# A two-layer transformer block on one core: attention operands in 64 rows a head, max and exp scores on opposite row halves, causal mask by extra rows, eight heads per value bank

## The reference

```python
x = x + 0.5 * moe(layernorm(x))          # 8 experts, top 2, capacity 193 a sequence
x = x + attention(layernorm(x))          # below
x = x + 0.5 * moe(layernorm(x))

q, k, v = x @ Wq + bq, x @ Wk + bk, x @ Wv + bv      # 16 heads of 8 columns
scores = q k^T / sqrt(8) + slope[head] * -|kpos - qpos|
scores = where(kpos > qpos, -inf, scores)
out = softmax(scores) v @ Wo + bo
```

## Time and profile before

| What | Value |
|---|---|
| median of 3 runs | 1056.23 us (1055.88 to 1057.18) |
| the profiled execution, first to last instruction | 1056.2 us |
| TensorE busy | 954.3 us, 90% |
| DVE busy | 776.1 us, 73% |
| ACT busy | 660.2 us, 63% |
| POOL busy | 603.5 us, 57% |
| attention, first score matmul to last value matmul | 192.6 to 885.0 us |

### The profile page before, as it was taken

One profiled execution on the slowest core, in us unless ns is written; L12 is line 12 of the kernel. 1 busy time (PEld: TensorE's weight loads), 2 busy tenths in 40 slices (PEclk: granted clock), 3 DMA queues, 4 the chain that ended last, 5 costly groups with the idle time before them and its releaser, 6 DMA issues. The chain is left out here.

```text
span 1056.2 us, 26705 instructions
## 1 busy us (share of the span) xinstructions
PE 954.3 (90%) x6880; PEld 501.3 (47%) x6880; DVE 776.1 (73%) x2596; ACT 660.2 (63%) x1570; POOL 603.5 (57%) x1220
## 2 busy tenths in 40 slices
PE   5999993689999989989998998999999996899997
PEld 2444441345555545455554554554555543444443
DVE  5999983677677767767876876776677732799996
ACT  4767763146676746657666675675666674577675
POOL 3777775236646635556464563654646343477777
PEclk9999996799999989999999998999999999899999
DMA  6500001434223223141231421323224001010011
GB/s 170 129 0 0 0 0 44 112 86 121 66 57 103 78 66 91 36 117 53 70 91 47 107 76 48 91 63 90 78 45 112 11 1 22 11 31 21 29 30 40
DMA packets 78828, 64.50 MB, mean 61 GB/s; under 512 B 9818, under 2 KB 78426, under 8 KB 78426
## 3 DMA queue, kind: packets, MB, share of 16 engines
q1 hardware_dynamic: 78734, 63.19, 22.8%
HBM read 33.54 MB, written 29.36 MB: 60 GB/s over the span
## 5 line engine op out<-in xcount | busy, mean ns | idle before, releaser
L1062 DVE TENSOR_REDUCE att_neg_max<-att_max 128x1 bf16<-128x384 f32 (+3 forms) x704 | 424.1, 640 | 164.0 <-PE att_max L865 163.8
L960 ACT ACTIVATE att_probs<-att_exp 128x512 f32<-128x512 f32 x640 | 358.7, 598 | 224.8 <-PE att_exp L883 223.7
L1026 POOL TENSOR_SCALAR_AFFINE_SELECT att_probs<-att_probs 128x256 f32<-128x256 f32 (+1 forms) x640 | 229.9, 363 | 314.3 <-ACT att_probs L960 306.3
L862 PE MATMUL att_max<-att_k_st,att_q_st 114*128 114x128 bf16 (+3 forms) x1024 | 278.5, 310 | 34.2 <-DMA att_k_st<-qk_parts 15.7
L883 PE MATMUL att_exp<-att_q_st,att_k_st 116*128 116x256 bf16 (+3 forms) x1024 | 245.6, 303 | 1.1 <-ACT att_probs L960 1.0
L865 PE MATMUL att_max<-bf_consts 128*128 128x128 bf16 x1024 | 200.3, 225 | 0.0
L862 PEld LDWEIGHTS att_max<-att_k_st,att_q_st 114*128 114x128 bf16 x1024 | 101.1, 99 | 202.9 <-issue 84.6
L900 PE MATMUL att_pv<-att_probs,att_v 128*32 128x512 f32 (+3 forms) x2048 | 191.6, 446 | 1.2 <-POOL att_probs L1026 1.2
L344 ACT ACTIVATE moe_scaled<-moe_hi,moe_gates 128x128 f32<-128x128 f32 x512 | 146.1, 372 | 59.3 <-PE moe_hi L290 58.9
L504 DVE SCALAR_TENSOR_TENSOR x<-moe_lo,moe_gates,x 128x128 f32 (+1 forms) x512 | 160.5, 338 | 18.9 <-PE moe_lo L284 17.9
L284 PE MATMUL moe_lo<-moe_we,moe_hT 128*128 128x512 f32 x256 | 135.1, 610 | 0.0
(11 more groups left out here) (77 smaller groups left out, 923.1 us busy)
## 6 DMA issues: line engine op xcount, KB each, us to landing
qk_parts<-att_parts SPq DMA_DIRECT2D x192, 128.0 KB, 2.3
att_q_st<-qk_parts SPq DMA_DIRECT2D x32, 384.0 KB, 3.9
att_k_st<-qk_parts SPq DMA_DIRECT2D x64, 192.0 KB, 4.3
x<-in_L_attn_x SPq DMA_DIRECT2D x16, 256.0 KB, 3.0
out<-x SPq DMA_DIRECT2D x16, 256.0 KB, 2.3
att_k_st<-zero_rows SPq DMA_DIRECT2D x4, 384.0 KB
moe_we<-in_L_ffn_We SPq DMA_DIRECT2D x2, 512.0 KB, 4.3
att_q_st<-att_shift SPq DMA_DIRECT2D x64, 4.0 KB, 2.9
```

What stands on the lines that cost most here:

```text
L862: nc.tensor.matmul(max_ps[m % RING][:, c * width:(c + 1) * width], q_st[par][0:MAX_K, r, i * P:(i + 1) * P], k_st[par][ab][0:MAX_K, r, 0:w ...
L960: nc.scalar.activation(probs[g % 2][:, n, :], exp_ps[m % RING][:], ACT.Exp).then_inc(exp_done, 1)
L1026: nc.gpsimd.affine_select(out=view, in_=view, compare_op=ALU.is_ge, fill=0.0, base=0, pattern=[[0, len(blocks)], [1, P]], channel_multipli ...
L1062: nc.vector.tensor_reduce(neg_max[par][:, g // 2, ab:ab + n_ab, r0:r0 + n_r, i].rearrange("p a r -> p r a"), max_ps[m % RING][:, 0:len(hea ...
```

## The change

Each head gets 64 rows of its own: 48 of parts, 3 of position, 11 for the mask inside a diagonal block, 1 for the mask of later blocks, 1 for the maximum. The even heads stand in partitions 0 to 63 and the odd ones in 64 to 127 of q_st, and of the two stacks k_max and k_exp. The 11 and 1 mask rows are built of powers of two, so that the identity matmul goes; max scores ahead of the diagonal block are a matmul with 51 rows, those of the diagonal block one with 62, and exp scores have 64. A group now is four heads of one side: in group g the exp pass takes side g % 2 and the max pass the other side. The units run from the widest to the narrowest. The values of the two sides of a head pair stand 16 columns apart in a 32-wide strip, so that eight heads are summed into one bank over two groups, with a turn and a copy for two groups. POOL clears diagonal blocks with 4 selects of 512 elements a group. The value bias goes through Wo once, ahead of the steps, and joins the output bias. A half stack is six DMAs of 48 rows. Turns and splits have other slots.

```diff
...
 Q_PARTS = [0, 0, 0, 1, 1, 2]
 K_PARTS = [0, 1, 2, 0, 1, 0]
 HEAD_ROWS = len(Q_PARTS) * HD
-ALIBI_ROW = 2 * HEAD_ROWS
-STEP_ROW = ALIBI_ROW + 3
-STEP = 32
-STEPS = S // STEP - 1
-SHIFT_ROW = STEP_ROW + STEPS
-MAX_K = SHIFT_ROW
-ALL_K = SHIFT_ROW + 2
+ALIBI_ROW = HEAD_ROWS
+FINE_ROW = ALIBI_ROW + 3
+FINE = 12
+FINES = -(-P // FINE)
+FAR_ROW = FINE_ROW + FINES
+SHIFT_ROW = FAR_ROW + 1
+SIDE = 64
+assert SHIFT_ROW + 1 == SIDE
 PAIRS = H // 2
...
+        group, within = at // FINE, at % FINE
+        fine = np.arange(FINES)[:, None]
+        k_fine = np.where(group == fine, -(2.0 ** (10 * within)), 0.0)
+        q_fine = np.where(group == fine, 2.0 ** (4 - 10 * within), np.where(group < fine, 2.0 ** 14, 0.0))
+        k_far = -(2.0 ** np.round(0.43 * (np.arange(S) - S // 2) - 15))
+        q_far = 2.0 ** np.round(-0.43 * (np.arange(S) - S // 2) - 15)
...
 SIDE_WORK = [
-    {2: "shift_hi", 5: "turn_o2"},
-    {1: "turn_h", 4: "project_q", 6: "turn_o3", 8: "project_k"},
-    {0: "turn_o", 3: "shift_lo", 5: "turn_o0", 7: "project_v"},
-    {0: "output", 5: "turn_o1"},
+    {2: "shift_hi"},
+    {1: "turn_h", 3: "turn_o1", 5: "project_q", 8: "project_k"},
+    {0: "turn_o", 3: "shift_lo", 6: "project_v"},
+    {1: "output", 3: "turn_o0"},
 ]
...
+MASK_UNITS = 4
...
 def max_unit(n):
-    return [(0, [0, 1, 2, 3]), (1, [0, 1]), (1, [2, 3]),
-            (2, [0]), (2, [1]), (2, [2]), (2, [3]), (3, [0]), (3, [1]), (3, [2]), (3, [3])][n]
+    return [(3, [0]), (3, [1]), (3, [2]), (3, [3]), (2, [0]), (2, [1]), (2, [2]), (2, [3]),
+            (1, [0, 1]), (1, [2, 3]), (0, [0, 1, 2, 3])][n]
 def exp_unit(n):
-    pair, u = divmod(n, 5)
-    return pair, [[(0, 0, 0)], [(0, 1, 0), (0, 3, 3 * P)], [(0, 2, 0), (1, 2, 2 * P)],
-                  [(1, 0, 0)], [(1, 1, 0), (1, 3, 3 * P)]][u]
+    if n < 4:
+        return [(n, 0, 0)]
+    if n < 8:
+        return [(n - 4, 1, 0), (n - 4, 3, 3 * P)]
+    return [(2 * (n - 8), 2, 0), (2 * (n - 8) + 1, 2, 2 * P)]
...
-        self.k_st = [[sb(f"k_st{i}{ab}", [P, PAIRS, S], BF16) for ab in range(2)] for i in range(2)]
-        self.v = [sb(f"v{i}", [P, T, H, VW]) for i in range(2)]
+        self.k_max = [sb(f"k_max{i}", [P, PAIRS, S], BF16) for i in range(2)]
+        self.k_exp = [sb(f"k_exp{i}", [P, PAIRS, S], BF16) for i in range(2)]
...
         for i in range(2):
-            eng.dma_start(self.q_st[i][ALIBI_ROW:SHIFT_ROW], self.consts.q_rows).then_inc(self.rows_in, DMA)
             for ab in range(2):
-                k_st = self.k_st[i][ab]
-                eng.dma_start(k_st[ALIBI_ROW:ALL_K], self.consts.k_rows[ab]).then_inc(self.rows_in, DMA)
-                eng.dma_start(k_st[(1 - ab) * HEAD_ROWS:(2 - ab) * HEAD_ROWS],
-                              self.consts.zero_rows).then_inc(self.rows_in, DMA)
+                r = ab * SIDE
+                eng.dma_start(self.q_st[i][r + ALIBI_ROW:r + SHIFT_ROW], self.consts.q_rows).then_inc(self.rows_in, DMA)
+                eng.dma_start(self.k_max[i][r + ALIBI_ROW:r + FAR_ROW],
+                              self.consts.k_max_rows[ab]).then_inc(self.rows_in, DMA)
+                eng.dma_start(self.k_exp[i][r + ALIBI_ROW:r + SIDE],
+                              self.consts.k_exp_rows[ab]).then_inc(self.rows_in, DMA)
...
                     sp.wait_ge(exp_out, (b - 2) * NE + (hf + 1) * NE // 2)
                 pairs = slice(hf * PAIRS // 2, (hf + 1) * PAIRS // 2)
-                sp.dma_start(q_st[par][0:2 * HEAD_ROWS, pairs, :],
-                             scratch[par, 0, pairs].rearrange("r u t d s -> (u t d) r s")).then_inc(
-                    stack_in[par][hf], DMA)
-                for ab in range(2):
-                    sp.dma_start(k_st[par][ab][ab * HEAD_ROWS:(ab + 1) * HEAD_ROWS, pairs, :],
-                                 scratch[par, 1, pairs, ab].rearrange("r t d s -> (t d) r s")).then_inc(
-                        stack_in[par][hf], DMA)
+                for side, stacks in ((0, (q_st,)), (1, (k_max, k_exp))):
+                    for dst in stacks:
+                        for ab in range(2):
+                            sp.dma_start(dst[par][ab * SIDE:ab * SIDE + HEAD_ROWS, pairs, :],
+                                         scratch[par, side, pairs, ab].rearrange("r t d s -> (t d) r s")).then_inc(
+                                stack_in[par][hf], DMA)
...
                 width = (i + 1) * P
+                half_at, ab = g // 2, 1 - g % 2
                 for c, hh in enumerate(heads):
-                    r, ab = divmod(4 * g + hh, 2)
-                    nc.tensor.matmul(max_ps[m % RING][:, c * width:(c + 1) * width],
-                                     q_st[par][0:MAX_K, r, i * P:(i + 1) * P], k_st[par][ab][0:MAX_K, r, 0:width],
-                                     start=True, stop=False)
-                    mm = nc.tensor.matmul(max_ps[m % RING][:, (c + 1) * width - P:(c + 1) * width],
-                                          consts.ident_b, consts.future_b, start=False, stop=True)
+                    r, at, low = 4 * half_at + hh, c * width, ab * SIDE
+                    if i > 0:
+                        nc.tensor.matmul(max_ps[m % RING][:, at:at + width - P],
+                                         q_st[par][low:low + FINE_ROW, r, i * P:(i + 1) * P],
+                                         k_max[par][low:low + FINE_ROW, r, 0:width - P], start=True, stop=True)
+                    mm = nc.tensor.matmul(max_ps[m % RING][:, at + width - P:at + width],
+                                          q_st[par][low:low + FAR_ROW, r, i * P:(i + 1) * P],
+                                          k_max[par][low:low + FAR_ROW, r, width - P:width], start=True, stop=True)
                 mm.then_inc(max_out, 1)
...
+                                          k_exp[par][low:low + SIDE, r, j * P:(j + 1) * P],
+                                          q_st[par][low:low + SIDE, r, j * P:S], start=True, stop=True)
                 mm.then_inc(exp_out, 1)
             def weigh_values(b, par, g, j):
+                half_at, ab = divmod(g, 2)
                 if j == 0:
...
+                    pe.wait_ge(masked, b * NK + (g + 1) * MASK_UNITS)
+                    if ab == 0 and (g > 0 or after(b, 0)):
+                        pe.wait_ge(pv_read, b * HALVES + half_at)
                     if g == 0:
                         pe.wait_ge(side_read, use(b - 1, "project_v"))
                 for hh in range(4):
-                    pair, ab = divmod(hh, 2)
-                    n, c = next((n, c) for n in range(EXP_UNITS) for a, jj, c in exp_unit(n)[1]
-                                if exp_unit(n)[0] == pair and (a, jj) == (ab, j))
-                    mm = nc.tensor.matmul(pv_ps[VW * hh:VW * (hh + 1), j * P:S], v[par][:, j, 4 * g + hh, :],
-                                          probs[g % 2][:, n, c:c + S - j * P], start=(j == 0), stop=(j == T - 1))
+                    n, c = next((n, c) for n in range(EXP_UNITS) for h, jj, c in exp_unit(n) if (h, jj) == (hh, j))
+                    mm = nc.tensor.matmul(pv_ps[VW * hh:VW * (hh + 1), j * P:S], v[par][:, j, 4 * half_at + hh, ab, :],
+                                          probs[g % 2][:, n, c:c + S - j * P], start=(ab == 0 and j == 0),
+                                          stop=(ab == 1 and j == T - 1))
                 if j == T - 1:
                     mm.then_inc(pv_out, 1)
...
+            nc.tensor.matmul(side_ps[:, 0:D], bv_cols[:], w["wo"][:], start=True, stop=True).then_inc(bias_out, 1)
+            pe.wait_ge(bias_ready, 1)
             all_steps(pe, step)
...
-                if g > 0 or after(b, 0):
-                    act.wait_ge(turned, use(b + 1 if g == 3 else b, f"turn_o{(g - 1) % GROUPS}"))
+                if hf == 1:
+                    act.wait_ge(turned, use(b, "turn_o0"))
+                elif after(b, 0):
+                    act.wait_ge(turned, use(b, "turn_o1"))
                 nc.scalar.activation(oT[:], pv_ps[:], ACT.Copy).then_inc(pv_read, 1)
             def side(b, par, half, what):
-                if what in ("project_v", "output") or what[:-1] == "turn_o":
+                if what in ("project_v", "output", "turn_o0", "turn_o1"):
...
-                pieces = exp_unit(n)[1]
-                view = probs[g % 2][:, n, :].rearrange("p (a c) -> p a c", c=P)
-                blocks = [c // P for _, _, c in pieces]
-                view = view[:, 0:1, :] if len(blocks) == 1 else view[:, 0:blocks[1] + 1:blocks[1], :]
+                if n not in (3, 7, EXP_UNITS - 1):
+                    return
                 pool.wait_ge(exp_done, b * NE + (g * EXP_UNITS + n + 1))
                 pool.sem_inc(pool_passed, 1)
-                nc.gpsimd.affine_select(out=view, in_=view, compare_op=ALU.is_ge, fill=0.0, base=0,
-                                        pattern=[[0, len(blocks)], [1, P]], channel_multiplier=-1).then_inc(masked, 1)
+                group = probs[g % 2][:].rearrange("p n (a c) -> p n a c", c=P)
```

(29 more changed lines are left out.)

99 lines of the change are left out of this document (54 added, 45 removed).

## The result

The changed kernel takes 1020.57 us in the median (1017.22 to 1026.38), the one before 1056.62; the ratio is 0.9656, with a 95% interval of 0.9612 to 0.97. So it is faster by 36 us, where 129 were forecast, and lies above the range of 903 to 1008. The profiled execution of the new kernel has a span of 1018.9 us.

The account below looks back on a forecast made before the run. TensorE was taken to set the 41.1 us step, DVE 10 us behind; 15 steps shortened to 32.2 save 133.5 us. With last steps -2, first steps +5, value bias +1.5: 1056.2 becomes 927 us, range 903 to 1008.

Parts of the forecast that it names:

- The stack's cover: Half-stack loads at each step's end: slack of some 7 us loses 3 and 2.5, still covering by 1.5 us.
- rival 4: The stack lands late in every step, 2 us over its cover; step above 34, 955 us; chance 0.08.
- The clock: At the loop boundary, short stretches at 1.2 GHz after some of five 3 us standstills; taken to stay.
- The coupling: TensorE and DVE through rings of three banks: starving costs 2 us a step (0.4 to 3.6), giving 32.2.
- The overlap: Max scores on one half of the array's rows run beside exp scores on the other: -7.2 us a step.
- Rivals 1 and 3: 1: halves don't run side by side, 1007 us, chance 0.15. 3: each passage between halves drains TensorE, 1184 us, 0.08.
- Rival 2: Loads of a half's second matmul show, up to 7 us a step; time 940 to 1000 us; chance 0.05.
- 0.1 a block: TensorE's 8 side blocks pay for the change of tiling mode: 0.1 us each, +0.8 us a step.
- The diagonal matmul: Masking by rows removes 64 matmuls with the mask constant from TensorE: -3.8 us a step.
- DVE, POOL and ACT: Work per step after the change: DVE 30.2 us busy, POOL about 19, ACT 26.8.
- The first steps: TensorE's two waits for the stack, 13.7 and 2.0 us, each grow by 2.5: +5 us in all.
- The loop boundary: 3 us of standing still at five places, with short stretches at 1.2 GHz after some; taken to stay.

Follow-up runs that it names:

- e3: The changed kernel with the two k_exp DMAs of each half stack issued behind everything else of the step, with their own semaphore; 959.17 us.
- e4: The changed kernel with 14 matmuls over 384 columns ahead of the wait for the stack in group 0 of every step; 996.54 us.
- e12: e5 with 6 full-height matmuls over 384 columns ahead of the wait for the normalised rows at slot 1 of group 1; 948.9 us.
- e5: The changed kernel with one k stack for both passes, a coarse mask in steps of 48 and 4 DMAs a half stack; 954.0 us.
- e10: e5 with ACT's exponential over the first 256 columns of each unit and DVE's one-head reductions over the last 128 columns; 931.4 us.
- e8: e5 with the max pass of a group on the same side as its exp pass, so that nothing overlaps; 1019.5 us.
- e1: The kernel before without the matmul of the identity and the -1e30 constant, so diagonal blocks are not masked in the max pass; 990.4 us.
- e7: e5 with the layer norm of sequence b + 2 one to two slots earlier; 957.5 us.

## Why the prediction was wrong

**The stack's cover.** This is the step that failed: "That slack of some 7 us shrinks with the step by 13 x 9/41, 3 us, and by 2.5 of more to issue and land. It still covers, by 1.5 us." The time between the stack's issue and the end of the step did not shrink by 3 us but by 5.4 (11.6 to 6.2). The splits that the stack waits for are POOL's and take as long as ever: counted from the turned rows, the last one ended after 14.6 us before, and ends after 15.2 now in steps at full clock. All that follows them got shorter: the next half's first issue came after 28.6 us and now comes after 23.8. And landing takes 8.4 us from the first issue in the median of 12 steps, where it took 5.2: its six pieces land 1.1 us apart with the DMA engines full. So of 6.4 us of cover, 5.4 and 3.2 went, and 2.2 are missing, where 1.5 were to be left over. This was rival 4 in kind, at 0.08 and 955 us. Its size was off too, because of the next point. Together the change and e3 differ by 4.3 us a step, 61 us.

**The clock.** The forecast had "short stretches at 1.2 GHz after some; they stay". Waits of mostly 1.5 to 2.9 us for the stack and of 1.2 at the turn, in each step, took it from 20.5 to 114 us in 13 steps. No term and no rival had it. Filled waits (e4, e12) measured it: 24 us behind the stack, 5 us on top of e5. By the mean step, e5 stands 0.9 us above e12, the waits for the stack in its first steps included.

**The coupling.** "I take 2 us: a step of 32.2" should have been a step of 34.6: +2.4. The sum had nothing for waits ahead of side work beyond those 2 us, and they are 1.9; and the score slots hold TensorE for 14.9 where it had 10.8 + 1.4 = 12.2. The bound was misplaced too: DVE isn't kept nearly full (29.3 of 34.6), and a third less work for it gives 0.3 us. It holds TensorE where full-width reductions follow one another at the end of a group (e10). The rest of the score slots' excess stays open. The max-only step, which I read as proof that DVE can be kept full, has one reader and nearly nothing between its slots.

**The overlap.** Right in mechanism, forecast at 7.2 us a step; between e8 and e5 it is worth 3.8. TensorE's score slots get 4.8 us shorter by it, and 0.9 of that goes into longer waits ahead of side work. "The queue is in order, so an exp matmul starts only when the unit's last max matmul has" was wrong, to the change's advantage: 572.75 against 572.86. Rivals 1 and 3 are out: halves run side by side, and a passage between halves costs nothing that shows. Rival 2 is out as well: a slot with four loads takes 0.23 us, the time of its 512 columns of exp scores. The Trainium skill's rule in TensorEngine Tiling (Array Packing), Key Properties, that a change of tiling mode drains TensorE, is in line with the rows. Eight side matmuls went from 0.98 to 1.10 us, project_q from 0.91 to 1.06 at full clock in e3, project_k from 0.86 to 1.06. I had 0.1 a block; it is 0.05 to 0.20, and 1.0 a step for 0.8.

**Smaller terms.** The diagonal matmul: 3.8 forecast, 3.0 measured alone (e1), the rest idle. DVE, POOL and ACT: right to 0.5 us. The first steps: +5 forecast; the two steps ahead of sequence 0 took 31.0 and 33.8 us for 28.3 and 30.1, +6.4, with TensorE at half clock through the whole max-only step. The loop boundary: "they stay" was wrong; the gap of 3 us is not seen apart from the stack's wait in the change, and not at all in e12. Here the miss was in the change's favour, by 42.7 - 41.1 = 1.6 us a step.

**The sum.** 2.4 (coupling and overlap) + 4.3 (stack and its clock) + 0.9 (the half clock that e5 still has) = 7.6 us a step, by 15 steps 114 us; less 1.6 by 13, 21 us, for the loop boundary: 93, and 1020.6 - 927 is 94. The parts of the first two terms among themselves are less sure than the sum: the experiments change one thing at a time on kernels that differ in others.

## What to carry to other kernels

When a change speeds up an engine that has no gaps, list every chain that runs beside it and doesn't speed up, and measure its cover in the shortened step by absolute times, from its last fixed producer to the step's end; a share of the step is the wrong measure. Of several loads that one wait covers, keep on the path only what is read first: the exp pass needed its k a step later, and moving two DMAs behind the others gave 61 us. And where the engine's clock falls after a wait of a microsecond or two, price the clock with the wait; if the wait can't go, empty matmuls in it may pay, which a run should confirm.

## What the runs showed of the hardware

Matmuls on the two halves of the array's rows run side by side at full rate (e10: 512 and 512 columns in 0.23 us), start 0.01 us apart, and one half can start ahead of a matmul of the other half that was issued before it. One after another they take 0.44 (e8).

The granted clock fell from 2.4 to 1.2 GHz at waits of 1.2 to 4.3 us in a TensorE that was else busy, for 3.4 or 6.8 us. It did so at 25 of the change's 26 such waits, and behind only 5 of the 13 waits of 1.1 us at e5's turn. In e1, where TensorE waits 0.8 us in each step, it didn't fall, but in e7 it did at 4 of 13 waits of 0.6 to 0.7 us. In the max-only step of the change the granted clock was 0.50 for all 33 us, with TensorE busy 28.81 of them; before, it was 1.00 from 8 us after the step's first matmul on (0.86 in the mean), with TensorE busy 23.11 of 28.30. The two differ in rows and in the diagonal matmuls, and which of that counts wasn't tried.

The kernel before stood still for 3 us at each turn of its loop; the kernel without the diagonal matmul did not. The cause wasn't tried further.
